# Two stacked LSTM layers in one kernel: the second runs 18 steps behind the first instead of 19, and the scan waits for one semaphore raised by two engines

## The chip, the cores and the metric

One Trainium2 chip, one of its cores. The metric is the device time of one execution in microseconds (us); less is better. The profile of one execution and the times of three others are given.

## What is computed

The reference takes x (2 sequences of 2048 tokens, 512 features, float32) and a condition vector for each sequence, and adds four layers to x, one after the other:

```python
x = x + L0(x, cond)   # low-rank layer made from cond, one 512x512 product per token
x = x + L1(x, cond)   # tanh(x @ W_ih.T + a term of cond)
x = x + L2(x, cond)   # LSTM over 2048 steps, h0 = cond
x = x + L3(x, cond)   # LSTM over 2048 steps, h0 = cond

def step(carry, xp_t):                      # both LSTMs
    prev_h, prev_c = carry
    h_bar = xp_t + prev_h @ Wh              # Wh: 512 x 2048
    i, f, o = (sigmoid(h_bar[:, k*512:(k+1)*512]) for k in range(3))
    g = tanh(h_bar[:, 3*512:])
    next_c = f * prev_c + i * g
    next_h = o * tanh(next_c)
    return (next_h, next_c), next_h
```

The projection xp = x @ Wx + b of an LSTM can be made ahead for many tokens, the product with Wh only step by step. L3's input at a token is L2's output at that token, so L3 can run beside L2 if it stays behind it.

## The kernel before, in words

`condition` makes the matrices of L0 and L1. Then `layers_and_recurrence` runs L0 and L1 on tiles of 256 tokens and both LSTMs. The LSTM called L2 in the code (index 0) is the third layer, L3 (index 1) the fourth.

Time is cut into chunks of CH = 16 steps. At step s of chunk c, L2 treats token 16c + s and L3 the token LAG = 19 earlier (`layers(s)`, `place`, `count`). At every step each engine emits L2's part and then L3's. In the first 19 steps only L2 is active, in the last 19 only L3; between them every step holds both. The 128 chunks are emitted as four in front, a hardware loop of 3 turns of 40 chunks, and the rest behind; chunk 128 and three steps of chunk 129 hold the end of L3.

One layer step:

- TensorE waits for `r2` (the state is ready) and multiplies the state, cut into three bf16 parts, with Wh: 48 matmuls of 512 columns, four at a time side by side in 32-column strips (`matmuls`, recorded as L80). The last raises `mm`.
- VectorE transposes the result (L1054, L1055, L1062), adds parts and projection (L1059, L1061, L1068), computes f*c (L1065), runs the scan that makes the new cell state (L1072), then after `between` h = o*tanh(c) (L1081) and the bf16 parts (L1085, L1088), the last of which raises `r2`.
- ScalarE copies the step's projection beside the sums (L941, raises `xp`), and computes sigmoid(f), sigmoid(i), tanh(g), sigmoid(o), tanh(c) (L945, L946, L948, L950, L952).
- GpSimd adds the residual (`residual`, L983), and raises `res`, which VectorE's L1081 of the layer's next step waits for.

The projections are spread over the chunk. `SUMS` says how many sums (one sum: 8 recorded matmuls, `project`, L874) stand at each step: for L3's next chunk 8 at s = 0 and 8 at s = 1, for L2's chunk ahead 2 at s = 2 and s = 3 and then one per step. `beside` puts half of a step's sums behind L2's matmuls and half behind L3's. Four sums make a quarter of a chunk's projection. VectorE transposes a finished quarter in `between` (`turn_quarter`, L1023), GpSimd adds the bias (`add_bias`, L992) and raises `ready`; `done_before` says at which layer step. ScalarE waits for quarter 3's `ready` before the first copy of a chunk. L3's chunk starts at s = 3 (19 = 16 + 3); quarter 3, summed beside L3 at s = 1, is transposed at L2's s = 2. Where only one layer is active, TensorE fills with `keep_warm`: 8 sets of dummy matmuls less the sums of the step (L884).

Finished output chunks are transposed at step `ROWS_AT` = LAG - 16 + 1 = 4 (`turn_rows`, L1031), and SyncE stores them with 8 DMAs.

Where two waits stand in front of an instruction, the built program of the kernel before has the first of them in the instruction and the second as an instruction of its own in front of it:

```
EventSemaphore    waits g  >= n
TensorTensorScan  waits fc >= n, raises c
```

(the scan, L1072; likewise `xp` in front of L1059 and `res` in front of L1081).

Of the kernel before, what the change touches and what calls it, by code (L numbers as in the profile page):

```python
# [28 lines left out]
ALU = mybir.AluOpType  # L29
ACT = mybir.ActivationFunctionType  # L30
# [3 lines left out]
NB = 2  # L34
# [3 lines left out]
NH = 4  # L38
# [7 lines left out]
HB = NH * NB  # L46
# [6 lines left out]
CH = 16  # L53
NCH = T // CH
# [3 lines left out]
NS = 1  # L58
# [536 lines left out]

LAG = CH + 2 + 1

ROWS_AT = LAG - CH + 1

BODY = 40  # L600
# [3 lines left out]
X2 = 4  # L604
L2, L3 = 0, 1
assert BODY % X2 == 0 and (NCH - X2) % BODY == X2


class Chunk:
# [29 lines left out]

    def count(self, l, s):  # L640

        return self.v * (BODY * CH) + (self.i * CH - LAG * l + s + 1)

# [21 lines left out]
    def done_before(self, l, s):  # L665


        layers = self.layers(s)
        if l != layers[0]:
            found = self.beside(layers[0], s)  # L670
        elif s:
            found = self.beside(self.layers(s - 1)[-1], s - 1)
        else:
            last = Chunk(self.v, self.i - 1)
            layers = last.layers(CH - 1)

            found = last.beside(layers[-1], CH - 1) if layers else last.sums(CH - 1)
            found = [(x, d - 1, q, h) for x, d, q, h in found]
        return [x[:3] for x in found if x[3] == NH - 1]


def layers_and_recurrence(nc, ins, keep, turn, pool_stream, cut_done, x1_dram, out):
    cond_t = keep["cond_t"]
    PAIR = (L2, L3)
    with ExitStack() as ctx:
# [43 lines left out]
        def blocks_of(s):  # L729
# [4 lines left out]

        names = ("mm", "xp", "trans_if", "trans_g", "trans_o", "pre_if", "pre_g", "pre_o", "f", "g", "fc", "c", "tanh", "h", "r1", "r2", "res",
                 "proj", "turn", "ready")
# [44 lines left out]
        with nc.Block() as block:  # L781
            @block.sync
            def _(sp):
# [23 lines left out]
                def emit(t):  # L807
                    if t.number == 1:
                        last_tiles()
                    if t.load_r:  # L810

                        sp.wait_ge(S[L2]["res"], t.count(L2, 0))
# [27 lines left out]
            def _(pe):  # L840
# [15 lines left out]
                def project(l, t, d, q, h):  # L856

                    if h == 0:
                        if q == 0 and l == L3 and t.number == 1:

                            pe.wait_ge(tiles.s_x1, NH * NTILE)
                        if q == 0 and l == L2:
                            pe.wait_ge(s_x1p[t.slot(d)], (t.half(d) + 1) * DMA)
                        if q == 0 and l == L3:
                            pe.wait_ge(S[L2]["res"], t.at(d + 1) * CH + 1)
                        if t.reused(d, q):
                            pe.wait_ge(S[l]["turn"], t.quarters(d, q) - 2)
# [66 lines left out]
            def _(act):  # L934
                def emit(t):
                    for s in range(t.steps):
                        for l in t.layers(s):
                            d, i = t.place(l, s)
                            if i == 0:
                                act.wait_ge(S[l]["ready"], t.quarters(d, 3))  # L940
                            act.copy(gates_t[l][:, :, 0:NS * NB], xp[l][:, t.slot(d), i, :].rearrange(  # L941
                                "p (m b) -> p m b", b=NS * NB)).then_inc(S[l]["xp"], 1)
                            n = t.count(l, s)
                            act.wait_ge(S[l]["pre_if"], n)
                            act.activation(gate_if[l][:, 1, :, 1], pre[l][:, HB:2 * HB], ACT.Sigmoid).then_inc(S[l]["f"], 1)  # L945
# [6 lines left out]
                            act.activation(tanh_c[l][:, :], g_c[l][:, :, 1], ACT.Tanh).then_inc(S[l]["tanh"], 1)  # L952
                        if t.number == 0:
# [22 lines left out]
            def _(pool):  # L976
                def residual(l, t, s):
# [6 lines left out]
                                       part(state[l], 0).rearrange("p h (b o) -> p h b o", o=1),  # L984
                                       ALU.add).then_inc(S[l]["res"], 1)

# [22 lines left out]
                pool.sem_inc(S[L2]["res"], 1)  # L1009
                pool.sem_inc(S[L3]["res"], 1)  # L1010
                for q in range(4):
# [4 lines left out]
            def _(dve):  # L1016
# [9 lines left out]
                def turn_rows(t, d):  # L1026

                    i = t.slot(d)
                    dve.wait_ge(S[L3]["res"], t.at(d + 1) * CH + 1)
                    dve.wait_ge(s_out[i], (t.half(d) + 1) * OUT)  # L1030
# [9 lines left out]
                def emit(t):  # L1040
                    for step in range(t.steps):
                        for l in t.layers(step):
                            s = S[l]
                            st = state[l]
                            n = t.count(l, step)

# [6 lines left out]
                            dve.wait_ge(s["mm"], n)  # L1053
                            dve.transpose(gates_t[l][:, 0:gf, NS * NB:], banked[:, 0:gf]).then_inc(s["trans_if"], 1)  # L1054
                            dve.transpose(gates_t[l][:, gf:ifg, NS * NB:], banked[:, gf:ifg]).then_inc(s["trans_g"], 1)  # L1055

# [4 lines left out]
                            dve.tensor_reduce(sums[:, gf:ifg], terms[:, gf:ifg], AXX, ALU.add).then_inc(s["pre_g"], 1)  # L1061
                            dve.transpose(gates_t[l][:, ifg:, NS * NB:], banked[:, ifg:]).then_inc(s["trans_o"], 1)  # L1062

                            dve.wait_ge(s["f"], n)
                            dve.tensor_tensor(g_fc[l][:, :, 1], gate_if[l][:, 1, :, 1], g_c[l][:, :, 1],  # L1065
                                              ALU.mult).then_inc(s["fc"], 1)
                            dve.wait_ge(s["trans_o"], n)
                            dve.tensor_reduce(sums[:, ifg:], terms[:, ifg:], AXX, ALU.add).then_inc(s["pre_o"], 1)  # L1068

                            dve.wait_ge(s["fc"], n)  # L1070
                            dve.wait_ge(s["g"], n)
                            dve.tensor_tensor_scan(g_c[l][:, :, :].rearrange("p n two -> p (n two)"),  # L1072
# [9 lines left out]
                                              tanh_c[l][:, :].rearrange("p (h b) -> p h b", h=NH),  # L1082
                                              ALU.mult).then_inc(s["h"], 1)
                            dve.wait_ge(s["h"], n)
                            dve.tensor_tensor(part(st, 1), part(st, 0), upper(part(st, 0)),  # L1085
                                              ALU.subtract).then_inc(s["r1"], 1)
                            dve.wait_ge(s["r1"], n)
# [108 lines left out]
```

## Time and the profile before

| | us |
|---|---|
| median of 3 runs | 11900.89 |
| lowest, highest | 11898.32, 11901.08 |
| the profiled execution | 11900.05 |
| its span in the profile | 11898.2 |
| PE busy | 11828.7 (99% of the span) |
| DVE busy | 8509.1 (72%) |
| ACT busy | 3758.9 (32%) |
| POOL busy | 1418.6 (12%) |

PE is TensorE, PEld its weight loads, DVE VectorE, ACT ScalarE, POOL GpSimd, SP SyncE. Matmuls overlap in the array: one is recorded as 379 ns although four start within some 216 ns. So a stretch of matmuls is judged by how far its start is from the next stretch's start.

### The profile page before, as it was taken

Reading aid. Unit: us, or ns where it says so; the run is one execution under the profiler, and the core shown is the slowest. Engines: PE = TensorE matmul, PEld = TensorE weight load, DVE = VectorE, ACT = ScalarE, POOL = GpSimd, SP = SyncE. Lnnn points to the kernel's source line nnn. Section 1 sums busy time; section 2 is a strip of 40 time slices with the busy share of each in tenths; the row PEclk is TensorE's granted clock in tenths of the full one; section 3 lists DMA queues with packets and bytes.
Section 4 is the critical chain, followed back from the end, with each engine's and each line's share of the span. In section 5 each row is a group of like instructions: output and inputs, shape, how many; then the busy total and the mean of one; then the engine's idle time right before and its main releaser. Section 6 shows DMA issues by size and latency. Waiting matters only on the chain.

```text
span 11898.2 us, 435945 instructions
## 1 busy us (share of the span) xinstructions
PE 11828.7 (99%) x231604; PEld 2698.0 (23%) x100532; DVE 8509.1 (72%) x46342; ACT 3758.9 (32%) x24698; POOL 1418.6 (12%) x5238
## 2 busy tenths in 40 slices
PE   8999999999999999999999999999999999999999
PEld 5222222222222222222222222222222222222222
DVE  2677777777777777777777777777777777777776
ACT  2233333333333333333333333333333333333332
POOL 4011111111111111111111111111111111111110
PEclk9999999999999999999999999999999999999999
DMA  4000000000000000000000000000000000000000
GB/s 164 25 4 5 4 5 4 5 5 4 5 5 4 5 5 4 5 4 5 4 5 5 4 5 5 4 5 5 4 5 4 5 4 5 5 4 5 5 5 3
DMA packets 374546, 107.86 MB, mean 9 GB/s; under 512 B 349594, under 2 KB 357830, under 8 KB 372436
## 3 DMA queue, kind: packets, MB, share of 16 engines
q1 hardware_dynamic: 362372, 61.96, 2.8%
q8 instruction: 1310, 21.46, 0.7%
q0 software_dynamic: 3504, 11.56, 0.3%
q14 instruction: 800, 6.55, 0.2%
q10 hardware_dynamic: 6560, 6.32, 0.2%
HBM read 62.98 MB, written 16.78 MB: 7 GB/s over the span
## 4 chain that ended last, share of the span: by engine, by line
PE 99%; DVE 0%; issue 0%; ACT 0%; POOLq 0%; POOL 0%; DVEq 0%
PE bank L80 89%; PE bank L874 7%; PE bank L518 1%; PE bank L531 1%; PE bank L484 0%; DVE gates_t L1055 0%; DVE gates_t L1062 0%; ACT gate_o L950 0%; DVE state L1085 0%; DVE state L1088 0%; DVE state L1081 0%; ACT tanh_c L952 0%; DVE pre L1068 0%; DVE pre L1061 0%; DVE g_fc L1065 0%
## 5 line engine op out<-in xcount | busy, mean ns | idle before, releaser
L80 PE MATMUL bank<-wh,state 128*6 128x512 bf16 x196608 | 11055.6, 379 | 20.8 <-DVE state L1088 20.8
L1054 DVE STREAM_TRANSPOSE gates_t<-bank 128x256 f32<-128x256 f32 x4096 | 1843.6, 450 | 2015.3 <-PE bank L80 2013.7
L80 PEld LDWEIGHTS bank<-wh,state 128*6 128x6 bf16 x65536 | 1568.1, 86 | 7400.5 <-issue 6498.0
L945 ACT ACTIVATE gate_if<-pre 128x8 f32<-128x8 f32 x4096 | 859.8, 210 | 7256.0 <-DVE pre L1059 7256.0
L1081 DVE TENSOR_TENSOR state<-gate_o,tanh_c 128x8 f32<-128x8 f32 x4096 | 688.2, 168 | 836.0 <-ACT tanh_c L952 811.2
L1062 DVE STREAM_TRANSPOSE gates_t<-bank 128x128 f32<-128x128 f32 x4096 | 1252.5, 306 | 0.0
L1055 DVE STREAM_TRANSPOSE gates_t<-bank 128x128 f32<-128x128 f32 x4096 | 1122.9, 274 | 0.0
L983 POOL TENSOR_TENSOR y<-x,state 128x8 f32<-128x8 f32 x2048 | 434.5, 212 | 5374.2 <-DVE state L1088 5374.2
L950 ACT ACTIVATE gate_o<-pre 128x8 f32<-128x8 f32 x4096 | 855.0, 209 | 642.8 <-DVE pre L1068 642.4
L983 POOL TENSOR_TENSOR x<-x1r,state 128x8 f32<-128x8 f32 x2048 | 434.5, 212 | 4961.2 <-DVE state L1088 4961.2
L952 ACT ACTIVATE tanh_c<-g_c 128x8 f32<-128x8 f32 x4096 | 854.7, 209 | 9.7 <-DVE g_c L1072 9.7
L874 PE MATMUL bank<-wx,x1p 128*32 128x128 f32 x16384 | 798.6, 273 | 1.5 <-DVE turned L1023 1.5
L948 ACT ACTIVATE g_fc<-pre 128x8 f32<-128x8 f32 x4096 | 793.0, 194 | 0.0
L946 ACT ACTIVATE gate_if<-pre 128x8 f32<-128x8 f32 x4096 | 792.8, 194 | 0.0
L1072 DVE TENSOR_TENSOR_SCAN g_c<-gate_if,g_fc 128x16 f32<-128x16 f32 x4096 | 785.4, 192 | 10.2 <-issue 10.2
L1085 DVE TENSOR_TENSOR state<-state 128x8 f32<-128x8 f32 x4096 | 691.0, 169 | 139.8
L1088 DVE TENSOR_TENSOR state<-state 128x8 f32<-128x8 f32 x4096 | 690.3, 169 | 139.7
L874 PEld LDWEIGHTS bank<-wx,x1p 128*32 128x32 f32 x16384 | 490.6, 110 | 1313.6 <-issue 982.0
L1061 DVE TENSOR_REDUCE pre<-gates_t 128x8 f32<-128x32 f32 x4096 | 763.5, 186 | 0.0
L1068 DVE TENSOR_REDUCE pre<-gates_t 128x8 f32<-128x32 f32 x4096 | 762.6, 186 | 0.0
L1059 DVE TENSOR_REDUCE pre<-gates_t 128x16 f32<-128x64 f32 x4096 | 726.8, 177 | 0.0
L1065 DVE TENSOR_TENSOR g_fc<-gate_if,g_c 128x8 f32<-128x8 f32 x4096 | 688.5, 168 | 2.0 <-issue 2.0
(124 smaller groups left out, 3490.6 us busy)
## 6 DMA issues: line engine op xcount, KB each, us to landing
w<-in_w SPq DMA_DIRECT2D x8, 2048.0 KB, 13.2
out<-y_rows SPq DMA_DIRECT2D x1020, 8.0 KB, 1.8
wx<-in_x SPq DMA_DIRECT2D x16, 512.0 KB, 5.4
x1p<-x_t_all SPq DMA_DIRECT2D x128, 64.0 KB, 2.6
x1r<-x_t_all SPq DMA_DIRECT2D x128, 64.0 KB, 2.6
x_t_all<-wx ACTq DMA_DIRECT2D x6, 1024.0 KB, 4.8
wx<-in_Wh POOLq DMA_DIRECT2D x8, 512.0 KB, 4.2
wx<-in_Wh POOLq DMA_DIRECT2D x16, 256.0 KB, 4.9
```

Source lines behind the costliest of these rows:

```text
L80: return pe.add_instruction(mybir.InstMatmult(name=nc.get_next_instruction_name(), engine=mybir.EngineType.PE, ins=[pe.lower_ap(moving), p ...
L874: mm = pe.matmul(proj[l][q % 2][C * j:C * j + C, 0:QN], tokens, w[:, j, QM * q:QM * q + QM, :], start=(h == 0), stop=(h == NH - 1), tile_p ...
L945: act.activation(gate_if[l][:, 1, :, 1], pre[l][:, HB:2 * HB], ACT.Sigmoid).then_inc(S[l]["f"], 1)
L946: act.activation(gate_if[l][:, 0, :, 1], pre[l][:, 0:HB], ACT.Sigmoid)
L948: act.activation(g_fc[l][:, :, 0], pre[l][:, 2 * HB:3 * HB], ACT.Tanh).then_inc(S[l]["g"], 1)
L950: act.activation(gate_o[l][:, :], pre[l][:, 3 * HB:], ACT.Sigmoid)
L952: act.activation(tanh_c[l][:, :], g_c[l][:, :, 1], ACT.Tanh).then_inc(S[l]["tanh"], 1)
L983: pool.tensor_tensor(dst[:, :, :, i:i + 1], src[:, :, :, i:i + 1], part(state[l], 0).rearrange("p h (b o) -> p h b o", o=1), ALU.add).then ...
L1054: dve.transpose(gates_t[l][:, 0:gf, NS * NB:], banked[:, 0:gf]).then_inc(s["trans_if"], 1)
L1055: dve.transpose(gates_t[l][:, gf:ifg, NS * NB:], banked[:, gf:ifg]).then_inc(s["trans_g"], 1)
L1062: dve.transpose(gates_t[l][:, ifg:, NS * NB:], banked[:, ifg:]).then_inc(s["trans_o"], 1)
L1072: dve.tensor_tensor_scan(g_c[l][:, :, :].rearrange("p n two -> p (n two)"), gate_if[l][:, 0, :, :].rearrange("p n two -> p (n two)"), g_fc ...
```

## The change

Two edits. LAG goes from 19 to 18, so L3's chunk starts at s = 2 and `ROWS_AT` becomes 3. In chunk 128 (`NCH`), where L3 is alone and all its sums stand beside L3's own steps, quarters 2 and 3 are transposed at s = 1 and no longer at s = 2, and there GpSimd adds the biases ahead of the residual.

The semaphores `g` and `fc` become one, `terms`, raised by 1 by tanh(g) on ScalarE and by 1 by f*c on VectorE; the scan waits for `terms` >= 2n. For VectorE to keep one register value for all its waits of a step, every semaphore that it waits for with that value is now raised by BOTH = 2 (`mm`, `xp`, `trans_*`, `f`, `tanh`, `h`, `r1`, `res`); `pre_*`, `c`, `r2` stay at 1.

```diff
-LAG = CH + 2 + 1
+LAG = CH + 2
+BOTH = 2
-    def count(self, l, s):
+    def count(self, l, s, each=1):
-        return self.v * (BODY * CH) + (self.i * CH - LAG * l + s + 1)
+        return self.v * (BODY * CH * each) + (self.i * CH - LAG * l + s + 1) * each
...
-        return [x[:3] for x in found if x[3] == NH - 1]
+        found = [x[:3] for x in found if x[3] == NH - 1]
+        if self.number == NCH:
+            own = [(L3, -1, 2), (L3, -1, 3)]
+            found = [x for x in found if x not in own] + (own if s == 1 else [])
+        return found
+    def own_turned(self, s):
+        return self.number == NCH and s == 1
...
-                            matmuls(l).then_inc(S[l]["mm"], 1)
+                            matmuls(l).then_inc(S[l]["mm"], BOTH)
...
-                            act.activation(g_fc[l][:, :, 0], pre[l][:, 2 * HB:3 * HB], ACT.Tanh).then_inc(S[l]["g"], 1)
+                            act.activation(g_fc[l][:, :, 0], pre[l][:, 2 * HB:3 * HB], ACT.Tanh).then_inc(S[l]["terms"], 1)
...
-                            residual(l, t, s)
-                            for x in t.done_before(l, s):
-                                add_bias(x[0], t, *x[1:])
+                            if t.own_turned(s):
+                                for x in t.done_before(l, s):
+                                    add_bias(x[0], t, *x[1:])
+                                residual(l, t, s)
+                            else:
+                                residual(l, t, s)
+                                for x in t.done_before(l, s):
+                                    add_bias(x[0], t, *x[1:])
...
-                            n = t.count(l, step)
+                            n = t.count(l, step, BOTH)
...
-                                              ALU.mult).then_inc(s["fc"], 1)
+                                              ALU.mult).then_inc(s["terms"], 1)
...
-                            dve.wait_ge(s["fc"], n)
-                            dve.wait_ge(s["g"], n)
+                            dve.wait_ge(s["terms"], n)
                             dve.tensor_tensor_scan(g_c[l][:, :, :].rearrange("p n two -> p (n two)"),
```

The other lines of the diff put BOTH for 1 in the raises and waits of the semaphores named above.

## Rows read from the trace of the kernel before

**Rows 1.** The page, busy time and share of each engine.

```profile
PE 11828.7 (99%) x231604; PEld 2698.0 (23%) x100532; DVE 8509.1 (72%) x46342; ACT 3758.9 (32%) x24698; POOL 1418.6 (12%) x5238
```

**Rows 2.** Waits over the whole span: total us, times, longest.

```profile
PE bank L80 <- DVE state L1088: 20.8, 23, 2.4
```

**Rows 3.** Windows: us, busy by engine, PEclk, DMA share, GB/s.

```profile
400.90:11791.70 11390.80, 11387.69 (x226888) 2458.39 (x97088) 8350.72 (x45760) 3640.71 (x24342) 1277.22 (x5063) 1.00 0.03 5
11804.90:11893.20 88.30, 76.36 (x1368) 20.48 (x815) 34.33 (x190) 15.25 (x101) 4.25 (x19) 1.00 0.01 3
...
11793.10:11795.10 2.00, 2.00 (x24) 0.14 (x4) 0.00 (x0) 0.00 (x0) 0.00 (x0) 0.50 0.00 0
```

**Rows 4.** The chain that ended last, 5580 to 5770: start, us, what.

```profile
5617.51 0.22 PE bank L874 x8
5617.73 5.18 PE bank L80 x96
...
5682.29 0.87 PE bank L874 x32
```

**Rows 5.** Timeline of one step with both layers, L3's chain: start, us, engine.

```profile
5640.14 0.19 ACT L948 ACTIVATE g_fc<-pre 128x8 f32<-128x8 f32 x1
5640.17 0.17 DVE L1065 TENSOR_TENSOR g_fc<-gate_if,g_c 128x8 f32<-128x8 f32 x1
...
5640.27 0.18 DVE L1068 TENSOR_REDUCE pre<-gates_t 128x8 f32<-128x32 f32 x1
5640.44 0.19 DVE L1072 TENSOR_TENSOR_SCAN g_c<-gate_if,g_fc 128x16 f32<-128x16 f32 x1
5640.49 0.21 ACT L950 ACTIVATE gate_o<-pre 128x8 f32<-128x8 f32 x1 [0.16 <-DVE pre L1068]
5640.66 0.21 ACT L952 ACTIVATE tanh_c<-g_c 128x8 f32<-128x8 f32 x1
...
5641.31 0.17 DVE L1088 TENSOR_TENSOR state<-state 128x8 f32<-128x8 f32 x1
5641.53 0.10 PEld L80 LDWEIGHTS bank<-wh,state 128*6 128x6 bf16 x4 [0.55 <-DVE state L1088]
```

**Rows 6.** Timeline around s = 2 of a chunk (L3's chain from 5609.13).

```profile
5608.89 0.46 POOL L992 TENSOR_TENSOR area<-turned,bias_all 128x128 f32<-128x128 f32 x1
...
5609.70 0.18 DVE L1059 TENSOR_REDUCE pre<-gates_t 128x16 f32<-128x64 f32 x1
...
5611.29 0.17 DVE L1088 TENSOR_TENSOR state<-state 128x8 f32<-128x8 f32 x1
...
5611.83 0.10 PEld L80 LDWEIGHTS bank<-wh,state 128*6 128x6 bf16 x4
```

**Rows 7.** Timeline of the end, L3 alone: chunk 128 from its s = 0.

```profile
11791.74 4.41 PE L80 MATMUL bank<-wh,state 128*6 128x512 bf16 x48 [2.42 <-DVE state L1088]
...
11802.78 0.51 DVE L1023 STREAM_TRANSPOSE turned<-bank 128x128 f32<-128x128 f32 x2
...
11803.15 1.96 PE L874 MATMUL bank<-wx,x 128*32 128x128 f32 x64 [1.80 <-DVE turned L1023]
...
11804.92 2.77 PE L80 MATMUL bank<-wh,state 128*6 128x512 bf16 x48
...
11809.13 0.51 DVE L1023 STREAM_TRANSPOSE turned<-bank 128x128 f32<-128x128 f32 x2
...
11810.15 2.76 PE L80 MATMUL bank<-wh,state 128*6 128x512 bf16 x48 [0.73 <-DVE state L1088]
...
11815.34 2.76 PE L80 MATMUL bank<-wh,state 128*6 128x512 bf16 x48 [0.70 <-DVE state L1088]
```

**Rows 8.** Timeline of the start, chunk 1: s = 2 and s = 3 of L2.

```profile
390.08 2.77 PE L80 MATMUL bank<-wh,state 128*6 128x512 bf16 x48
...
395.31 2.76 PE L80 MATMUL bank<-wh,state 128*6 128x512 bf16 x48 [0.72 <-DVE state L1088]
...
395.50 0.88 POOL L992 TENSOR_TENSOR area<-turned,bias_all 128x128 f32<-128x128 f32 x2
```

More of the change, by code:

```diff
@@ L733, in blocks_of @@
             return [(NFRONT + n // (2 * NH), n // NH % 2, n % NH) for n in units]
-        names = ("mm", "xp", "trans_if", "trans_g", "trans_o", "pre_if", "pre_g", "pre_o", "f", "g", "fc", "c", "tanh", "h", "r1", "r2", "res",
+        names = ("mm", "xp", "trans_if", "trans_g", "trans_o", "pre_if", "pre_g", "pre_o", "f", "terms", "c", "tanh", "h", "r1", "r2", "res",
                  "proj", "turn", "ready")
@@ L810, in emit @@
                     if t.load_r:
-                        sp.wait_ge(S[L2]["res"], t.count(L2, 0))
+                        sp.wait_ge(S[L2]["res"], t.count(L2, 0, BOTH))
                         load_x1(sp, x1r, t.slot(1), t.at(1), s_x1r)
@@ L864, in project @@
                         if q == 0 and l == L3:
-                            pe.wait_ge(S[L2]["res"], t.at(d + 1) * CH + 1)
+                            pe.wait_ge(S[L2]["res"], t.at(d + 1) * (CH * BOTH) + BOTH)
                         if t.reused(d, q):
@@ L951, in emit @@
                             act.wait_ge(S[l]["c"], n)
-                            act.activation(tanh_c[l][:, :], g_c[l][:, :, 1], ACT.Tanh).then_inc(S[l]["tanh"], 1)
+                            act.activation(tanh_c[l][:, :], g_c[l][:, :, 1], ACT.Tanh).then_inc(S[l]["tanh"], BOTH)
                         if t.number == 0:
@@ L984, in residual @@
                                        part(state[l], 0).rearrange("p h (b o) -> p h b o", o=1),
-                                       ALU.add).then_inc(S[l]["res"], 1)
+                                       ALU.add).then_inc(S[l]["res"], BOTH)
                 def add_bias(l, t, d, q):
@@ L1002, in emit @@
                                 pool.wait_ge(s_x1r[t.slot()], (t.half() + 1) * DMA)
[L1004 to L1006 removed]
+                            if t.own_turned(s):
[6 more added lines that the diff above has]
+                                    add_bias(x[0], t, *x[1:])
                 pool_stream(pool)
[L1009 to L1010 removed]
+                pool.sem_inc(S[L2]["res"], BOTH)
+                pool.sem_inc(S[L3]["res"], BOTH)
                 for q in range(4):
@@ L1028, in turn_rows @@
                     i = t.slot(d)
-                    dve.wait_ge(S[L3]["res"], t.at(d + 1) * CH + 1)
+                    dve.wait_ge(S[L3]["res"], t.at(d + 1) * (CH * BOTH) + BOTH)
                     dve.wait_ge(s_out[i], (t.half(d) + 1) * OUT)
@@ L1053, in emit @@
                             dve.wait_ge(s["mm"], n)
-                            dve.transpose(gates_t[l][:, 0:gf, NS * NB:], banked[:, 0:gf]).then_inc(s["trans_if"], 1)
-                            dve.transpose(gates_t[l][:, gf:ifg, NS * NB:], banked[:, gf:ifg]).then_inc(s["trans_g"], 1)
+                            dve.transpose(gates_t[l][:, 0:gf, NS * NB:], banked[:, 0:gf]).then_inc(s["trans_if"], BOTH)
+                            dve.transpose(gates_t[l][:, gf:ifg, NS * NB:], banked[:, gf:ifg]).then_inc(s["trans_g"], BOTH)
                             dve.wait_ge(s["trans_if"], n)
@@ L1061, in emit @@
                             dve.tensor_reduce(sums[:, gf:ifg], terms[:, gf:ifg], AXX, ALU.add).then_inc(s["pre_g"], 1)
-                            dve.transpose(gates_t[l][:, ifg:, NS * NB:], banked[:, ifg:]).then_inc(s["trans_o"], 1)
+                            dve.transpose(gates_t[l][:, ifg:, NS * NB:], banked[:, ifg:]).then_inc(s["trans_o"], BOTH)
                             dve.wait_ge(s["f"], n)
                             dve.tensor_tensor(g_fc[l][:, :, 1], gate_if[l][:, 1, :, 1], g_c[l][:, :, 1],
-                                              ALU.mult).then_inc(s["fc"], 1)
+                                              ALU.mult).then_inc(s["terms"], 1)
                             dve.wait_ge(s["trans_o"], n)
                             dve.tensor_reduce(sums[:, ifg:], terms[:, ifg:], AXX, ALU.add).then_inc(s["pre_o"], 1)
-                            dve.wait_ge(s["fc"], n)
-                            dve.wait_ge(s["g"], n)
+                            dve.wait_ge(s["terms"], n)
                             dve.tensor_tensor_scan(g_c[l][:, :, :].rearrange("p n two -> p (n two)"),
@@ L1082, in emit @@
                                               tanh_c[l][:, :].rearrange("p (h b) -> p h b", h=NH),
-                                              ALU.mult).then_inc(s["h"], 1)
+                                              ALU.mult).then_inc(s["h"], BOTH)
                             dve.wait_ge(s["h"], n)
                             dve.tensor_tensor(part(st, 1), part(st, 0), upper(part(st, 0)),
-                                              ALU.subtract).then_inc(s["r1"], 1)
+                                              ALU.subtract).then_inc(s["r1"], BOTH)
                             dve.wait_ge(s["r1"], n)
```

4 lines of the change are left out of this document (2 added, 2 removed).

## The prediction

> **What bounds the kernel now.** I read the page first: PE is busy for 99% of the span, the next engine for 72% [rows 1]. Matmul ends are modelled, so this alone proves little. The waits come next: PE's matmuls waited for the state (L1088) 23 times in all, 20.8 us together [rows 2]. There are 4096 layer steps, so in nearly all of them TensorE never waits for the recurrence. The windows by stage say where it does: from 400.9 to 11791.7 us, where both layers are active, PE is busy 11387.7 of 11390.8 us at full granted clock; in the end, where L3 is alone, 76.4 of 88.3 us, and part of that is dummy work [rows 3]. The chain that ended last, read in the middle, holds nothing but matmuls: 96 matmuls of two layer steps in 5.18 us, so 2.59 us each, one sum of a projection 0.22 us, four sums 0.87 us [rows 4]. A step of both layers therefore costs 5.18 us plus its sums, and 32 layer steps with 32 sums, which is one chunk, cost 32 x 2.59 + 32 x 0.22 = 89.9 us. Some 11390 of 11900 us are this stream, and only work taken off TensorE shortens it. Where one layer is alone, a step is the latency of matmuls and VectorE's chain one after the other: 11815.34 - 11810.15 = 5.19 us [rows 7].
>
> **The lag, from 19 to 18.** It takes no matmul of the recurrence away. It turns one step of L2 alone and one step of L3 alone into one step of both, and at both ends something else changes with it.
>
> Start. Now s = 2 of chunk 1 is L2 alone and takes 395.31 - 390.08 = 5.23 us, with 2 sums inside, which are free there [rows 8]. After, it holds both layers: 5.18 + 2 x 0.22 = 5.62 us. So L2 falls back by 0.39 us at the start. L3's first copy must wait for four biased quarters. GpSimd adds the last two in 0.88 us from 395.50, behind L2's residual, so `ready` stands at 396.38 [rows 8]; copy and hand-over take some 0.25 us (my estimate: 0.2 us is about one ScalarE instruction of this size, as L948 and L950 [rows 5], and 0.03 us from an end to the waiting start, as from the scan's end at 5640.63 to L952 at 5640.66), so L3's L1059 can start at 396.65. L3's matmuls would end around 395.7 and L1059 would stand 0.57 us later, at 396.27 (in rows 6 it stands at 5609.70, 0.57 us behind the chain's start at 5609.13). L3's chain is late by 0.4 us; its next matmuls come 2.81 us after the chain's start and the chain takes 2.33 us (5609.13 to 5611.46 [rows 6]), so 0.48 us of room, less the weight load of 0.1 us. I count 0.05 us. Once. Start: +0.44 us.
>
> End. One step of L3 alone goes: -5.19 us. But chunk 128 pays. At its s = 1 VectorE now transposes only quarters 0 and 1 (x2 at 11802.78), and the first of these lets TensorE start the 8 sums of quarters 2 and 3 at 11803.15, done at 11805.11, while VectorE goes on to the state; the matmuls of s = 2 follow the sums at 11804.92 with no gap [rows 7]. After the change VectorE's queue holds the transposes of quarters 2 and 3 in front of L1081, and they wait for those very sums. Behind them in VectorE's queue stand L1081, L1085 and L1088, and TensorE waits for these. Quarter 2 is summed halfway, near 11804.15, so its transpose fits in; its buffer's bias (quarter 0) was added by then, 0.46 us on GpSimd [rows 6] from about 11803.1. Quarter 3 is summed at 11805.11; its transpose, some 0.31 us (two take 0.51 and overlap), ends near 11805.45; and at s = 2 the matmuls started 11810.15 - (11809.13 + 0.51) = 0.51 us behind the end of the last transpose [rows 7]. So the matmuls of s = 2 start near 11805.96 instead of 11804.92: +1.04 us. The biases ahead of the residual on GpSimd end near 11805.9, the copy that waits for them is wanted 3.3 us after the matmuls' start, and the residual is wanted by the L1081 a step later: 0. The two transposes that leave s = 2 give 5.23 - 5.19 = 0.04 us back. End: -5.19 + 1.04 - 0.04 = -4.19 us.
>
> In between: 127 chunk starts. Quarter 3 is transposed at L2's s = 2 as before, but L3 wants it one step sooner, so its cover of 5.4 us (a step of both) is gone. GpSimd's bias ends at 5609.35; 0.25 us for hand-over and copy gives 5609.60 to 5609.65; L1059 would start at 5609.70 anyway [rows 6]. That is on time by under 0.1 us. Behind it lies a second cover: the chain ends at 5611.46 and TensorE loads L3's next weights at 5611.83 [rows 6], 0.37 us later, because a sum stands between. So 0 us, and a delay has to pass some 0.45 us to reach TensorE. `turn_rows` moves from L3's s = 4 to s = 3, where `between` holds nothing else; its transpose of the size of L1023 hides as that does, behind sigmoid and tanh on ScalarE. Its 8 stores on SyncE's queue come one step sooner; behind them stand the next chunk's two loads, which wait for later events, and DMA is 3% busy [rows 3]: 0.
>
> **The scan's wait.** In the plain step both inputs of the scan are there early: tanh(g) ends at 5640.33 and f*c at 5640.34, yet the scan starts at 5640.44. L1068, which has one wait, starts 0.10 us behind L1065; the scan, with a second wait as an instruction of its own, 0.17 us behind L1068 [rows 5]. With one wait it can start near 5640.37: 0.07 us sooner. Does ScalarE pass that on? L952 starts at 5640.66, before L950 ends (5640.70) and 0.03 us after the scan's end, so it is the scan that it waits for: yes, up to 0.07 us per step. But in the long middle it buys nothing: the state is ready at 5641.48, TensorE's load of it is at 5641.53 in the same 0.65 us rhythm as its neighbours, and the matmuls run on without a gap [rows 4, 5]. It counts only where a chain is waited for: 23 times now by matmuls [rows 2]. After the change I count 4 at the start (the last two steps of chunk 0, s = 0 and s = 1 of chunk 1) and 19 at the end (L3's last step beside L2 and its 18 alone, of which the last is followed by the output): 23 x 0.07 = -1.6 us. From below, the wait could cost nothing: 0. From above, 23 x 0.1 = -2.3 us, the scan starting with its inputs. I take 1.6.
> The Trainium skill, "VectorE: DVE Perf Modes", section "Rules for kernel authors", says for chained operations to minimise the count of operations and not of semaphores, and its section on the DRAIN that a semaphore costs nothing extra. By it this term is 0 and the time 1.6 us longer. The 0.17 against 0.10 us of rows 5 speaks against it, but the second wait is another case than a semaphore inside an instruction.
>
> **Raising by 2.** The trace has no compute instruction that raises by 2. DMAs raise by 16. Below: 0, one update as before. Above: each such raise needs an instruction of its own in the queue, at the 0.07 us of the extra wait. Five of them stand in VectorE's step (L1054, L1055, L1062, L1081, L1085), 0.35 us. I take 0, since a raise is a number in the instruction; the bound makes a rival. One register value per step on VectorE stays one: 0.
>
> **Sum.** +0.44 - 4.19 - 1.6 = -5.35 us. Against the profiled execution, 11900.05 (span 11898.2 and 1.85 around it): 11894.7. That execution lies 0.84 us under the median of 11900.89, and a median should stand to a median: 11895.5 us. That is 0.04% faster. Three runs spread over 2.8 us; a change under 0.2%, 24 us, is about what a measurement of this kernel can't tell from none.
>
> **Rivals.**
> - *The extra wait costs nothing*: the scan starts as late as before for another reason (its own start-up). 11895.5 + 1.6 = 11897.1. For it: no scan with one wait is in the trace. Chance 0.10.
> - *The clock falls in the end.* At 11791.74, after a gap of 2.42 us, the granted clock was 0.50 (1.2 GHz) for a while and 48 matmuls took 4.41 instead of 2.76 us [rows 3, 7]. After the change chunk 128 holds a new gap of about 0.9 us in front of s = 2, behind one of 1.8 us. One such fall costs 1.65 us: 11897.2. Against it: the gap of 1.80 us passed without a fall. Chance 0.08.
> - *L3's first copy is late in each chunk.* If GpSimd's bias or the copy takes 0.5 us more than I read, TensorE stands 0.05 us in each of 127 chunks: +6 us, 11902. To come out slower than 0.2% it must hold TensorE (24 + 5.3) / 127 = 0.23 us per chunk, so the projection must be 0.7 us late. For it: the time to spare is under 0.1 us at the first cover. Against it: the second cover. Chance 0.05, of which 0.015 beyond 24 us.
> - *Raising by 2 costs*, the other side. VectorE's chain grows from 2.33 to 2.68 us. In steps where no sum stands between, TensorE can give it only 2.59 us, so some 0.1 us is lost in half of the layer steps: 2048 x 0.1 = 205 us, 12100 us. It decides as soon as the chain grows by about 0.25 us. Against it: nothing in the trace makes a raise dearer by its size. Chance 0.025.
> The Trainium skill, "Trainium Kernel Development and Optimization", section "Key Constraints", says that compute semaphores are raised by 1; no trace here shows what a raise by 2 does, and its rule gives no price.
> - *Faster than 0.2%*: the middle would have to run 0.006 us per layer step quicker. PE is 99.97% busy there [rows 3], with nothing taken from it. Chance 0.015.
>
> **How the numbers follow.** The forecast has 0.73: 11895.5 us. The two small rivals lie 1.6 us above it, run-to-run spread adds 1.4 us on either side, the high bound of the scan 0.7 us below, and a few us of drift between chips I can't exclude. From 11888 to 11903 us holds the forecast, the first two rivals and the mild half of the third; beyond it are 5 to 10 in 100. Faster by over 0.2%: 0.015, slower: 0.015 + 0.025 = 0.04, the rest, 0.945, within.
>
> **What the profile after should show.** The scan 0.10 us behind L1068, not 0.17. L3's first copy of a chunk (L941 from the area buffer) held by GpSimd's L992 and starting near 0.3 us behind the start of VectorE's chain, and L1059 still 0.57 us behind it. The chain that ended last nothing but matmuls in the middle, a chunk 89.9 us. The plain steps of L3 alone at 5.12 us each. In chunk 128 a gap of about 0.9 us on TensorE in front of s = 2 that waits for VectorE. I am wrong if a chunk takes more than 89.9 us, or if matmuls wait for the state more than some 25 times.

## The result, and the profile after

The kernel became slower: 12070.8 us median of 4 runs (12066.9 to 12072.8) against 11900.7 us, a ratio of 1.0143 (95% interval 1.0127 to 1.0159), 170 us more. The forecast was 11895.5 us, in a range of 11888 to 11903. The profiled execution has a span of 12070.3 us at a granted clock of 0.999, as before, so it is not the clock. Two repeats of the experiments below (one of e4, one of e6) ran at a lower granted clock, and the times given leave them out.

Lines have moved: L1054, L1055, L1059, L1062, L1068, L1072, L1081, L1085, L1088 are now L1070, L1071, L1075, L1078, L1084, L1087, L1096, L1100, L1103; L941, L945, L948, L952 are L952, L956, L959, L963; L992 is L1003, L1023 L1039, L874 L885.

The page after, the row that answers to [rows 1]:

```profile
PE 11955.7 (99%) x231548; PEld 2705.9 (22%) x100476; DVE 8530.0 (71%) x46342; ACT 3889.2 (32%) x24698; POOL 1424.0 (12%) x5238
```

PE is still "99% busy", with 56 matmul records fewer and 127 us more of time. This share hides the loss: the modelled ends of matmuls fill gaps of a tenth of a microsecond. The waits of the kernel after (engine and line, what it waited for: us in total, times, longest) don't hide it:

```profile
PEld bank L80 <- DVE state L1103: 1383.3, 1819, 3.6
DVE state L1096 <- ACT tanh_c L963: 1274.0, 3465, 0.8
DVE gates_t L1070 <- PE bank L80: 1175.5, 2477, 4.4
ACT gates_t L952 <- POOL area L1003: 207.7, 128, 2.9
PE bank L80 <- DVE state L1103: 52.7, 135, 2.7
DVE pre L1075 <- ACT gates_t L952: 35.4, 124, 0.7
```

TensorE's matmuls waited 135 times for the state, not 23 [rows 2]. The third row says most. The same row of the waits before:

```profile
DVE gates_t L1054 <- PE bank L80: 2013.7, 4059, 4.5
```

Before, VectorE waited for TensorE (by more than 0.15 us, what this view counts) ahead of L1054 in 4059 of 4096 layer steps; now it waits in 2477. In the other some 1600 it is late itself, and VectorE, busy for 71% of the span, sets the pace. The row of L1075 is new: VectorE's first reduction of a chunk waits for ScalarE's first copy of L3's projection, and that copy for GpSimd's bias (the row above it). I call this the late copy.

The chain that ended last, in the middle, beside [rows 4]:

```profile
5636.75 5.23 PE bank L80 x96
5642.20 5.23 PE bank L80 x96
5647.65 5.23 PE bank L80 x96
```

5.45 us from pair to pair where 5.18 + 0.22 = 5.40 us stood. I took the spacing of all starts of L1070 from 480 to 11700 us (123 whole chunks): a chunk takes 91.19 us on average, before 89.90. Intervals without a sum, 12 in a chunk, take 2.64 to 2.68 us instead of 2.59; those with one take 2.81 to 2.84 instead of 2.81; the two behind L3's first copy take 2.94 and 2.92 instead of 2.81. 1.29 us in some 124 chunks is 160 us.

The timeline of a plain step after, beside [rows 5]; VectorE's chain starts at 5642.09:

```profile
5642.66 0.18 DVE L1075 TENSOR_REDUCE pre<-gates_t 128x16 f32<-128x64 f32 x1
...
5642.93 0.21 ACT L956 ACTIVATE gate_if<-pre 128x8 f32<-128x8 f32 x1 [1.57 <-DVE pre L1075]
...
5643.38 0.19 DVE L1087 TENSOR_TENSOR_SCAN g_c<-gate_if,g_fc 128x16 f32<-128x16 f32 x1
...
5643.67 0.21 ACT L963 ACTIVATE tanh_c<-g_c 128x8 f32<-128x8 f32 x1
...
5643.97 0.17 DVE L1096 TENSOR_TENSOR state<-gate_o,tanh_c 128x8 f32<-128x8 f32 x1 [0.39 <-ACT tanh_c L963]
...
5644.44 0.17 DVE L1103 TENSOR_TENSOR state<-state 128x8 f32<-128x8 f32 x1
```

Read the hand-overs, from an end to the start that waits for it. L1075 ends at 5642.84 and the sigmoid starts 0.09 us later; the scan ends at 5643.57 and tanh starts 0.10 us later; tanh ends at 5643.88 and L1096 starts 0.09 us later. Before, such a hand-over took 0.03 us (the scan's end to L952 [rows 5]). L1100 stands 0.27 us behind L1096, not 0.20. From 5642.09 to L1103's end at 5644.61 the chain takes 2.52 us, before 2.33. With 0.11 us from L1103's end to the next L1070 (the median where no sum stands between) that is 2.63 us: more than the 2.59 us of 48 matmuls.

Where L3 is alone nothing covers the chain, and its whole growth shows. VectorE's first transposes at the end of the run, timeline after:

```profile
12013.23 0.45 DVE L1070 STREAM_TRANSPOSE gates_t<-bank 128x256 f32<-128x256 f32 x1 [2.93 <-PE bank L80]
12018.67 0.45 DVE L1070 STREAM_TRANSPOSE gates_t<-bank 128x256 f32<-128x256 f32 x1 [2.93 <-PE bank L80]
```

A step alone takes 5.44 us. The forecast had 5.12, before it took 5.19 [rows 7].

The program as built names the instruction behind each 0.06 us. Waits are in brackets:

```
before                                        after
StreamTranspose [mm]      sem-inc 1           EventSemaphore  [mm]
                                              StreamTranspose []     sem-add-imm 2
EventSemaphore  [res]                         EventSemaphore  [res, tanh]
TensorTensor    [tanh]    sem-inc 1           TensorTensor    []     sem-add-imm 2
TensorTensor    [h]       sem-inc 1           EventSemaphore  [h]
                                              TensorTensor    []     sem-add-imm 2
TensorTensor    [r1]      sem-inc 1           TensorTensor    [r1]   sem-inc 1
Activation      [pre_if]  sem-inc 1           EventSemaphore  [pre_if]
                                              Activation      []     sem-add-imm 2
```

An instruction that raises by 1 holds its own wait. One that raises by 2 holds none; its wait stands in front of it as an instruction of its own. The trace after has no exception: of the 36864 instructions of VectorE, ScalarE and GpSimd that raise by 2 none holds a wait, of those that raise by 1 31036 do. So the change took one such instruction away (the scan's) and brought five: `mm` and `h` on VectorE, `pre_if` and `c` on ScalarE, `r2` on GpSimd; and `tanh`'s wait has left its instruction for the one that `res` had already. The page counts 452453 instructions, before 435945.

### The profile page after: what moved, and what is told of

It reads as the page before. It is cut to its first block, busy times and chain, and to the rows that moved or that the text cites. A ratio compares the mean times of both kernels' runs of the same rounds, so it can differ in the third digit from the quotient of the medians.

```text
span 12070.3 us, 452453 instructions
## 1 busy us (share of the span) xinstructions
PE 11955.7 (99%) x231548; PEld 2705.9 (22%) x100476; DVE 8530.0 (71%) x46342; ACT 3889.2 (32%) x24698; POOL 1424.0 (12%) x5238
## 4 chain that ended last, share of the span: by engine, by line
PE 92%; DVE 4%; issue 2%; ACT 1%; POOL 0%; DVEq 0%; ACTq 0%; POOLq 0%
PE bank L80 83%; PE bank L885 7%; PE bank L518 1%; PE bank L531 1%; DVE gates_t L1071 1%; ACT tanh_c L963 1%; DVE gates_t L1078 0%; DVE state L1100 0%; DVE state L1096 0%; DVE state L1103 0%; DVE g_fc L1081 0%; ACT gate_o L961 0%; DVE pre L1075 0%; DVE pre L1084 0%; DVE pre L1077 0%
## 5 line engine op out<-in xcount | busy, mean ns | idle before, releaser
L956 ACT ACTIVATE gate_if<-pre 128x8 f32<-128x8 f32 x4096 | 866.7, 212 | 7173.1 <-DVE pre L1075 7173.1
L1070 DVE STREAM_TRANSPOSE gates_t<-bank 128x256 f32<-128x256 f32 x4096 | 1844.8, 450 | 1313.3 <-PE bank L80 1175.5
L1096 DVE TENSOR_TENSOR state<-gate_o,tanh_c 128x8 f32<-128x8 f32 x4096 | 689.5, 168 | 1331.0 <-ACT tanh_c L963 1274.0
L1078 DVE STREAM_TRANSPOSE gates_t<-bank 128x128 f32<-128x128 f32 x4096 | 1253.9, 306 | 0.4
L1071 DVE STREAM_TRANSPOSE gates_t<-bank 128x128 f32<-128x128 f32 x4096 | 1124.7, 275 | 0.0
L1100 DVE TENSOR_TENSOR state<-state 128x8 f32<-128x8 f32 x4096 | 692.1, 169 | 443.5 <-DVE state L1096 24.5
L963 ACT ACTIVATE tanh_c<-g_c 128x8 f32<-128x8 f32 x4096 | 863.6, 211 | 19.8 <-issue 9.6
L885 PE MATMUL bank<-wx,x1p 128*32 128x128 f32 x16384 | 798.8, 273 | 1.5 <-DVE turned L1039 1.5
L959 ACT ACTIVATE g_fc<-pre 128x8 f32<-128x8 f32 x4096 | 797.6, 195 | 1.2
L1103 DVE TENSOR_TENSOR state<-state 128x8 f32<-128x8 f32 x4096 | 691.4, 169 | 147.4 <-DVE state L1100 8.9
L1087 DVE TENSOR_TENSOR_SCAN g_c<-gate_if,g_fc 128x16 f32<-128x16 f32 x4096 | 785.8, 192 | 9.5 <-ACT g_fc L959 4.5
L885 PEld LDWEIGHTS bank<-wx,x1p 128*32 128x32 f32 x16384 | 490.7, 110 | 1314.2 <-issue 985.9
L1077 DVE TENSOR_REDUCE pre<-gates_t 128x8 f32<-128x32 f32 x4096 | 761.7, 186 | 0.0
L1075 DVE TENSOR_REDUCE pre<-gates_t 128x16 f32<-128x64 f32 x4096 | 734.7, 179 | 35.4 <-ACT gates_t L952 35.4
L1084 DVE TENSOR_REDUCE pre<-gates_t 128x8 f32<-128x32 f32 x4096 | 736.3, 180 | 1.9 <-issue 1.9
L1081 DVE TENSOR_TENSOR g_fc<-gate_if,g_c 128x8 f32<-128x8 f32 x4096 | 692.7, 169 | 14.2 <-ACT gate_if L956 11.7
```

Source lines behind the costliest of these rows:

```text
L885: mm = pe.matmul(proj[l][q % 2][C * j:C * j + C, 0:QN], tokens, w[:, j, QM * q:QM * q + QM, :], start=(h == 0), stop=(h == NH - 1), tile_p ...
```

## The experiments

Of the runs below, e1 to e4 are of one chip and e5 to e10 of another; the kernel before took 11900.3 us on the first and 11900.1 and 11900.6 us on the second.

Theory A: waits in instructions of their own make the chain longer than TensorE covers. Rivals: the raise by 2 is slow in itself; the 18 steps cost; GpSimd's longer wait costs.

**e1, the lag alone.**

```diff
-LAG = CH + 2 + 1
+LAG = CH + 2
```

with the order in chunk 128 as in the change, and all semaphores as before.

> The lag alone: L3 is 18 steps behind, with the two own quarters of chunk 128 transposed at s = 1; every semaphore is raised by 1, g and fc stay apart. Theory 1 (the loss is all from raising by 2, because a wait that shared the instruction becomes an instruction of its own): 11897 us, 4 us under the kernel before; a chunk 89.9 us; L1054 to the end of L1088 2.33 us; in chunk 128 a gap of about 1 us in front of the matmuls of s = 2. Theory 2 (the lag costs: L3's first copy of a chunk is late and TensorE pays): L3's first sum of a chunk held by the copy by 0.2 to 0.3 us and up to 0.3 us x 127 = 36 us slower, 11935 us.

Measured: 11897.5 us, ratio 0.9998 (0.9989 to 1.0007). The forecast's sum for this part is 11900.9 - 3.75 = 11897. A chunk takes 89.91 us and matmuls wait 21 times. The end, timeline of e1:

```profile
11806.77 2.76 PE L80 MATMUL bank<-wh,state 128*6 128x512 bf16 x48 [1.03 <-DVE state L1100]
```

The gap that I put at 1.04 us is there. The lag alone costs nothing in the middle. Its gain of 3 us is within what can't be told from none.

**e2, the semaphores alone:** the changed kernel at 19 steps, with `done_before` and GpSimd's order as before.

```diff
-LAG = CH + 2
+LAG = CH + 2 + 1
```

> The semaphores alone: terms, and all raises by BOTH = 2, with the lag left at 19. Theory 1: the whole loss and a bit more, since the 4 us of the lag are missing: 12070 to 12080 us, tail steps of 5.44 us as in the changed kernel. Theory 2: the part of the lag is gone, 12035 us or less.

Measured: 12037.0 us, ratio 1.0115 (1.0099 to 1.0130): 2 us above Theory 2's bound, 33 below Theory 1's. The semaphores make 136 of the 170 us, and a chunk takes 90.90 us. The 18 steps bring 34 us on top, though by themselves (e1) they cost nothing.

**e3, one semaphore for the scan, all raises by 1:** e1 and `terms`, with a count of its own.

```diff
+                            n2 = t.count(l, step, 2) + l
-                            dve.wait_ge(s["fc"], n)
-                            dve.wait_ge(s["g"], n)
+                            dve.wait_ge(s["terms"], n2)
```

> The lag of 18 and the fused semaphore terms, with all raises by 1: the scan alone waits for twice the count (for L3 one more, so that its register is not kept for 18 steps), which costs VectorE one register instruction per layer step. Theory 1: 11895.5 us, the scan 0.10 to 0.12 us behind the reduction in front of it, steps of L3 alone 5.12 us. If the register instruction costs what a wait of its own costs, the gain of the scan is lost: 11897 us, 5.19 us.

Measured: 11890.9 us (11889.0 to 11897.9), ratio 0.9993 (0.9984 to 1.0002). VectorE's chain where L3 is alone, timeline of e3:

```profile
11832.76 0.45 DVE L1068 STREAM_TRANSPOSE gates_t<-bank 128x256 f32<-128x256 f32 x1 [2.86 <-PE bank L80]
...
11833.89 0.19 DVE L1082 TENSOR_REDUCE pre<-gates_t 128x8 f32<-128x32 f32 x1
11833.99 0.19 DVE L1085 TENSOR_TENSOR_SCAN g_c<-gate_if,g_fc 128x16 f32<-128x16 f32 x1
...
11837.89 0.45 DVE L1068 STREAM_TRANSPOSE gates_t<-bank 128x256 f32<-128x256 f32 x1 [2.86 <-PE bank L80]
```

The scan starts 0.10 us behind the reduction, and a step alone takes 11837.89 - 11832.76 = 5.13 us, not 5.19 [rows 7]. What the edit was to do, it does. The Trainium skill ("VectorE: DVE Perf Modes", section "The DRAIN you can't avoid") has a semaphore cost nothing extra. That agrees with waits inside instructions here: in the trace before, L1061, which holds one, starts 0.11 us behind L1059, and L1062, which holds none, 0.10 us behind L1061. It doesn't agree with a wait that stands alone, which was worth 0.07 us.

**e4, waits apart, raises by 1:** e3 with a wait on `r2`, long since true, ahead of five waits, so that each becomes an instruction of its own (`pre_if` and `c` on ScalarE; `mm`, `tanh`, `h` on VectorE). GpSimd's is left in its instruction.

```diff
+                            act.wait_ge(S[l]["r2"], n)
                             act.wait_ge(S[l]["pre_if"], n)
```

> As e3 (raises by 1), but five waits of each layer step are made instructions of their own, by a wait that is long true in front of each: pre_if and c on ScalarE, mm, tanh (with res) and h on VectorE. Theory 1 (the separate wait costs, not the raise): the time of the changed kernel, 12060 to 12085 us, and tail steps near 5.44 us. Rival (the raise by 2 is itself the cost): as e3, 11896 us.

Measured: 12073.7 us, ratio 1.0145 (1.0126 to 1.0163). With no raise by 2 at all, the changed kernel's time is back, with 132 waits of the matmuls and a chunk of 91.19 us, as after. The waits of e4:

```profile
DVE gates_t L1071 <- PE bank L80: 1184.7, 2481, 4.4
```

That is 2481 for 2477, and a step of L3 alone takes 5.44 us. GpSimd's extra instruction is not needed for the total. That the totals agree to 3 us is in part luck, for it is made up differently: with GpSimd's wait inside its instruction the late copy is rarer (VectorE waits for it 17 times, not 124, and the two intervals behind it take 2.86 and 2.89 us, not 2.94 and 2.92), while the intervals without a sum take 2.66 to 2.69 us, not 2.64 to 2.68.

**e5, raises by 2 without waits:** e3 with `mm`, `xp`, `trans_g` and `trans_o` raised by 2. The instructions that raise them hold no wait, so none is put apart.

```diff
-                            matmuls(l).then_inc(S[l]["mm"], 1)
+                            matmuls(l).then_inc(S[l]["mm"], 2)
```

> As e3, but four semaphores are raised by 2 where the raising instruction carries no wait of its own: mm (the last of 48 matmuls), xp, trans_g and trans_o. Theory 1 (only a displaced wait costs): the time of e3, 11891 us, within 3 us, and the waits for these four start as late as in e3. Rival (a raise by 2 is slower to arrive): mm and xp come later by some 0.06 us each, steps of L3 alone 5.12 + 0.06 = 5.18 us.

Measured: 11890.8 us, ratio 0.9992 (0.9982 to 1.0001), e3's time; a step of L3 alone takes 5.12 us, not 5.18. So the raise by 2 is free where it displaces no wait. Its price is only that it displaces one.

**e6 and e7, how many such waits are covered:** e4 with ScalarE's two alone, and with VectorE's three alone.

> As e3, but the two waits of ScalarE for pre_if and c are instructions of their own. VectorE's chain grows by 0.12 us, from 2.26 to 2.38 us, which is still about what the kernel before had. Theory 1 with a threshold (TensorE gives the chain about 2.5 us before it waits): nothing in the middle, 0.12 us in some 22 steps with one layer, 11893 to 11896 us. Rival without a threshold (the loss goes with the number of waits, 183 us for five): 2/5 of it, 11960 us.

> As e3, but the three waits of VectorE for mm, for tanh with res, and for h are instructions of their own. The chain grows by 0.19 us to 2.45 us, just under the 2.5 us. Theory 1 with a threshold: 11895 to 11905 us. Rival without a threshold: 3/5 of 183 us, 12000 us.

Measured: e6 11911.5 us, ratio 1.0011 (1.0001 to 1.0021); e7 11934.2 us, ratio 1.0030 (1.0018 to 1.0041). Over e3 that is 21 and 43 us, against 183 us for all five (e4). So there is a threshold, but a soft one: both numbers missed, by 16 and 29 us, and both rivals' by 49 and 66. Where nothing covers the chain the waits simply add up: a step of L3 alone takes 5.12 us in e3, 5.24 in e6, 5.32 in e7 and 5.44 in e4, and 0.12 + 0.20 = 0.32. Timelines, first of e3, then e6, then e7, from the scan to the state:

```profile
5643.39 0.19 DVE L1085 TENSOR_TENSOR_SCAN g_c<-gate_if,g_fc 128x16 f32<-128x16 f32 x1
5643.61 0.20 ACT L959 ACTIVATE tanh_c<-g_c 128x8 f32<-128x8 f32 x1
5643.85 0.17 DVE L1094 TENSOR_TENSOR state<-gate_o,tanh_c 128x8 f32<-128x8 f32 x1 [0.28 <-ACT tanh_c L959]
```

```profile
5641.54 0.19 DVE L1087 TENSOR_TENSOR_SCAN g_c<-gate_if,g_fc 128x16 f32<-128x16 f32 x1
5641.82 0.21 ACT L961 ACTIVATE tanh_c<-g_c 128x8 f32<-128x8 f32 x1
5642.07 0.17 DVE L1096 TENSOR_TENSOR state<-gate_o,tanh_c 128x8 f32<-128x8 f32 x1 [0.34 <-ACT tanh_c L961]
```

```profile
5642.78 0.19 DVE L1086 TENSOR_TENSOR_SCAN g_c<-gate_if,g_fc 128x16 f32<-128x16 f32 x1
5643.01 0.20 ACT L959 ACTIVATE tanh_c<-g_c 128x8 f32<-128x8 f32 x1
5643.30 0.17 DVE L1096 TENSOR_TENSOR state<-gate_o,tanh_c 128x8 f32<-128x8 f32 x1 [0.33 <-ACT tanh_c L959]
```

0.46, 0.53 and 0.52 us from the scan's start to L1094/L1096's, in e4 and after 0.58: one instruction more, 0.06 us more, on whichever engine it stands. Over the steps without a quarter to transpose the median chain takes 2.27 us in e3, 2.39 in e6, 2.39 in e7 and 2.52 in e4, and from the end of one to the start of the next VectorE needs 0.05 us (an estimate: e4's 0.11 less the 0.06 of the wait for `mm`), or with a wait for `mm` 0.11: 2.32, 2.44, 2.50 and 2.63 us against 2.59. Only e4 is over. Chunks take 89.88, 90.01, 90.14 and 91.19 us. The threshold is where the sum says. What e6 and e7 lose below it are single steps (in e6 the intervals without a sum take 2.60 us on average and up to 2.74), for e7 in part at fixed places of the program (last section). Why the others run long stays open.

**e8, the bias ahead of the residual at every step:** to take the late copy out of the changed kernel.

```diff
-                            if t.own_turned(s):
+                            if True:
```

> The changed kernel, but GpSimd adds the bias of a finished quarter before the residual of the same step, everywhere and not only in chunk 128, so that L3's projection is ready some 0.9 us sooner. Theory (of the loss of 170 us, about 33 us are L3's late first copy of a chunk, which the longer chain and GpSimd's own separate wait uncover): 12070.8 - 37 = 12034 us, L1075 never held by the copy. Rival (the whole loss is the chain's length): 12070 us.

Measured: 12138.6 us, ratio 1.0200 (1.0183 to 1.0217): 68 us worse, where I expected 37 better. The copy is no longer late (L1075 never waits for it; the two intervals take 2.86 and 2.83 us, not 2.94 and 2.92). The cost is new. Timeline of e8:

```profile
5654.02 0.21 ACT L963 ACTIVATE tanh_c<-g_c 128x8 f32<-128x8 f32 x1
...
5654.30 0.47 POOL L1003 TENSOR_TENSOR xp<-turned,bias_all 128x128 f32<-128x128 f32 x1 [1.79 <-DVE turned L1039]
5654.32 0.46 DVE L1096 TENSOR_TENSOR state<-gate_o,tanh_c 128x8 f32<-128x8 f32 x1
```

L1096 takes 0.17 us elsewhere. Here it starts 0.02 us behind GpSimd's sum and ends with it. Over the run, groups of instructions by line, after and then e8 (busy us, mean ns):

```profile
L1096 DVE TENSOR_TENSOR state<-gate_o,tanh_c 128x8 f32<-128x8 f32 x4096 | 689.5, 168 | 1331.0 <-ACT tanh_c L963 1274.0 <-issue 1.4
```

```profile
L1096 DVE TENSOR_TENSOR state<-gate_o,tanh_c 128x8 f32<-128x8 f32 x4096 | 932.8, 228 | 1326.9 <-ACT tanh_c L963 1271.4 <-issue 0.2
```

243 us more: 968 of the 4096 take 0.37 to 0.47 us. The residual that GpSimd now does later is not the cost, for the idle time ahead of L1096 has not grown (1326.9 us against 1331.0). Behind the residual, as in the changed kernel, the same sum falls beside VectorE's transposes, which keep their 0.45 and 0.27 us.

**e9, the bias ahead for one quarter of eight**, the one whose copy is late.

```diff
-                            if t.own_turned(s):
+                            if t.own_turned(s) or any(x[0] == L3 and x[2] == 3 for x in t.done_before(l, s)):
```

> The changed kernel, with GpSimd's bias sum put ahead of its residual for one quarter in each chunk only: the third layer's last, whose sum the first copy of a chunk waits for. Theory 1: this late copy is what the 18 steps cost beside the long chain. In the run with the bias first everywhere the two turns behind it took 2.86 and 2.83 us against 2.94 and 2.92, and the one ahead 0.01 more, so 0.16 us in each of 124 chunks is given back: about 12051 us (12045 to 12056), and VectorE's first reduction no longer waits for the copy. Theory 2: the 34 us of the 18 steps lie elsewhere: 12070 us. If the sum that is moved ahead holds VectorE up where it now falls, by the 0.29 us seen in L1096, as much is lost as gained: 12075 to 12085.

Measured: 12041.4 us, ratio 1.0118 (1.0101 to 1.0134). L1075 never waits for the copy, the mean of L1096 is 174 ns, and a chunk takes 90.96 us. So moving this one sum gives back 29 of the 34 us that the 18 steps brought on top of e2. I had taken 20, from the two intervals behind the copy, and these do take what they took in e8 (2.86 and 2.83 us). The rest is spread over the other intervals of a chunk in hundredths of a microsecond; why is not shown.

**e10, e3 with the bias ahead everywhere.**

```diff
-                            if t.own_turned(s):
+                            if True:
```

> The kernel with raises by 1, 18 steps and the terms counted by themselves, now with the bias sum ahead of the residual for all eight quarters of a chunk. Theory 1: what cost 68 us with the long chain is VectorE's L1096, that takes 0.46 us in place of 0.17 beside GpSimd's sum of 0.47 us; with the short chain a turn has some 0.2 us to spare, so at most 0.1 us is left of each: 11891 to 11990 us, likeliest near 11910, and the mean of VectorE's state sum is near 228 ns again and not 168. Theory 2: the 68 us come from the residual sum that GpSimd does later, a wait of VectorE on it: then they show as idle time ahead of that line, its mean stays 168 ns, and the time is 11891 us or 11950 us by whether the short chain covers it.

Measured: 11894.5 us, ratio 0.9994 (0.9985 to 1.0004), 3.6 us over e3 and not told from it. L1094's mean is 168 ns, against theory 1's line. The collision has moved by one instruction, as the timeline of e10 shows:

```profile
5658.78 0.17 DVE L1094 TENSOR_TENSOR state<-gate_o,tanh_c 128x8 f32<-128x8 f32 x1
5658.89 0.46 POOL L999 TENSOR_TENSOR xp<-turned,bias_all 128x128 f32<-128x128 f32 x1 [2.06 <-DVE turned L1036]
5658.98 0.39 DVE L1098 TENSOR_TENSOR state<-state 128x8 f32<-128x8 f32 x1
5659.40 0.17 DVE L1101 TENSOR_TENSOR state<-state 128x8 f32<-128x8 f32 x1
```

L1098 has a mean of 212 ns over 4096, in e3 169: 176 us (0.043 x 4096) of VectorE's time that the short chain's slack takes up, where the long chain's 243 us cost 68.

## Why the prediction was wrong

**The failed step is "Raising by 2 ... I take 0, since a raise is a number in the instruction".** It is true of the raise (e5) and wrong of the instruction, which then has no place for its wait. The text even knew the two things that it failed to put together: that of two waits one stands in the instruction and one in front, and that the one in front costs 0.07 us. The question to ask was what else the raising instruction has to hold. The runs show 0.06 us for each, on VectorE and on ScalarE. The chain grew from 2.33 to 2.52 us, plus 0.06 for `mm`; a step of L3 alone took 5.44 us and not 5.12, five times 0.064; and the term that I put at 0 was worth 136 us by itself (e2).

**The rival on the other side had the mechanism**, "the chain grows by about 0.25 us" and TensorE gives it 2.59 us, at 12100 us and a chance of 0.025. Two things in it were off. Its bound put an instruction at five raises of VectorE and none elsewhere; built were three places on VectorE, one of them joined with an older wait, and two on ScalarE that lie on the same chain. And the loss is 1.00 us a chunk (e2), not 0.1 us in 16 of 32 layer steps: 12 intervals of a chunk have no sum, and they lose 0.05 to 0.09 us. The slack was nearer 0.2 us: 2.33 + 0.05 against 2.59. That its 12100 us lies near the measured time is in part luck: it priced the chain at 1.6 us a chunk and had nothing of the 34 us of the late copy. The chance was far too low for a cost that I had bounded at 200 us and had no row against.

**The lag.** Start and end came out about as summed: e1 took 11897.5 us for 11897, and the gap in chunk 128 was 1.03 us for 1.04. The single parts are less exact than that: in the profile of e1 chunks 1 and 2 together take 0.48 us more (0.44 forecast), and all from chunk 127 on 5.4 us less (4.2 forecast). "So 0 us" in the middle was right for the chain of 2.33 us and wrong for the longer one: the "second cover" of 0.37 us was made of the same slack that the waits had used up. Timeline after, at s = 2, beside [rows 6]:

```profile
5686.35 0.45 DVE L1070 STREAM_TRANSPOSE gates_t<-bank 128x256 f32<-128x256 f32 x1 [0.29 <-PE bank L80]
5686.37 0.47 POOL L1003 TENSOR_TENSOR area<-turned,bias_all 128x128 f32<-128x128 f32 x1
...
5686.93 0.22 ACT L952 COPY gates_t<-area 128x32 f32<-128x32 f32 x1 [1.60 <-POOL area L1003]
5687.25 0.22 DVE L1075 TENSOR_REDUCE pre<-gates_t 128x16 f32<-128x64 f32 x1 [0.25 <-ACT gates_t L952]
```

L1075 stands 0.90 us behind the chain's start, not 0.57: GpSimd's sum starts 0.02 us behind that start, where [rows 6] have it 0.24 us ahead. The first cover, which I called "under 0.1 us", is gone. So the third rival came true in a form that it did not have: it wanted the projection 0.7 us late to cost over 24 us, and 0.33 us late was enough once the waits had used the second cover. By themselves the two parts of the change come to 136 us (e2) and -3 us (e1); together they cost 170.

**The scan's wait.** 0.07 us was right (e3: 0.10 us behind the reduction, 5.13 us a step). e3 comes out at 11890.9 for a sum of 11895.5, within what can be told. But from e1 to e3, which differ by this wait and a register operation, the medians fall by 6.6 us and not 1.6; in the two profiles 4 us of it lie in the middle (89.91 and 89.88 us a chunk), where I had said that it buys nothing. Whether that is the wait or the spread of single runs is not shown.

**The signs.** I had named a chunk of more than 89.9 us and more than 25 waits as what would make me wrong. Both came. The second rival's fall of the clock did not: behind the new gap in chunk 128, 1.20 us in the trace after, the 48 matmuls took 2.76 us, as ahead of the change [rows 7].

The best version is e3: the same idea with a count of its own for the new semaphore, some 9 us under before in the medians and not told from it by its interval. For that it spends a register operation in a layer step, and the raises stay at 1.

## What to carry to other kernels

Before changing what a semaphore is raised by, look in the built program at every instruction that raises it: if it has a wait, a raise by 2 puts that wait in front of it, and here that was 0.06 us on the chain each time the engine had to wait for it. Keep a second count in a register before you scale the raises. And when two edits lean on the same slack in a chain, price the second one with the first one's cost already taken out.

## What the runs showed beside it

- A wait in an instruction of its own costs where what it waits for has only just happened: 0.03 us of hand-over become 0.09 to 0.10 us, on VectorE and ScalarE alike, and 0.06 to 0.07 us even where it is the engine's own last instruction (`h`). One such instruction holds two waits (`res` and `tanh`), and its second wait adds nothing that shows.
- With VectorE's waits apart, some steps start L1096 0.3 to 0.4 us late with nothing in the profile to wait for. Of the 2954 steps in which VectorE transposes nothing between the scan and L1096, these are 51 after (16 us in all), 28 in e7 (10 us) and 28 in e4, and none before, in e1, e3, e5, e6 or e10. 48 of the 51 are 16 places of the loop in each of its 3 turns; one of them is at 1599.53, 5246.18 and 8892.80 us, timelines after:

```profile
5246.18 0.19 DVE L1087 TENSOR_TENSOR_SCAN g_c<-gate_if,g_fc 128x16 f32<-128x16 f32 x1
5247.05 0.17 DVE L1096 TENSOR_TENSOR state<-gate_o,tanh_c 128x8 f32<-128x8 f32 x1 [0.68 <-ACT tanh_c L963]
...
8892.80 0.19 DVE L1087 TENSOR_TENSOR_SCAN g_c<-gate_if,g_fc 128x16 f32<-128x16 f32 x1
8893.67 0.17 DVE L1096 TENSOR_TENSOR state<-gate_o,tanh_c 128x8 f32<-128x8 f32 x1 [0.68 <-ACT tanh_c L963]
```

  3646.6 us apart, which is 40 chunks, one turn. That points to the loading of instructions. The DMA packets of the trace go with it: in all 51 a packet of the instruction queue that the page lists as q14 starts 2.4 to 3.1 us behind the chain's start, and in 75 of 2781 other such steps from 480 to 11700 us. Which comes first stays open.
- VectorE's product or difference of 8 columns takes 0.31 to 0.47 us instead of 0.17 while GpSimd adds 128 columns (0.47 us), as if it had to wait for it; its transposes beside the same sum don't get longer.
